# Gated attention's output projection and linear layer as three-pass products of split halves, the third norm on ScalarE, and two context buffers that swap homes

## The reference, cut to what matters

```python
# layer 2: gated linear attention
xb = silu(causal_conv(x)); q = xb @ Wq; k_gate = xb @ Wkg; v = xb @ Wv; g = xb @ Wg + bg
...
o = (o - mu) * lax.rsqrt(var + EPS)              # per head
out = jax.nn.silu(g) * o @ Wout                  # the output projection
# layer 3: linear layer with quantised operands, blocks of 32
xd = (xq * xs[..., None]).reshape(x2.shape)
wd = (wq * ws[..., None]).reshape(w2.shape)
out = xd @ wd.T + bias                           # the linear layer
# layer 4: cross attention, 16 heads
q = split(query @ Wq + bq); k = split(key @ Wk + bk); v = split(value @ Wv + bv)
...
x = x + layer(_layernorm(x, axis=-1))            # around each layer
```

## Time and profile before

| what | us |
|---|---|
| median of 3 runs (lowest, highest) | 1195.95 (1195.74, 1195.97) |
| the profiled execution's own time | 1191.81 |
| its span in the profile | 1190.5 |
| outside the span (1191.81 - 1190.5) | 1.3 |
| granted clock of PE over the span | 0.996 of full speed |
| PE, DVE, ACT, POOL busy | 1143.4, 744.6, 536.0, 236.7 |
| the loop: first scores to the end of the last linear product | 245.9 to 360.4 |

### The profile page before, as it was taken

One profiled execution on the slowest core, in us unless ns is written; L12 is line 12 of the kernel. 1 busy time (PEld: TensorE's weight loads), 2 busy tenths in 40 slices (PEclk: granted clock), 3 DMA queues, 4 the chain that ended last, 5 costly groups with the idle time before them and its releaser, 6 DMA issues.

```text
span 1190.5 us, 21697 instructions
## 1 busy us (share of the span) xinstructions
PE 1143.4 (96%) x8729; PEld 848.7 (71%) x8729; DVE 744.6 (63%) x1505; ACT 536.0 (45%) x1032; POOL 236.7 (20%) x292
## 2 busy tenths in 40 slices
PE   7999999989989999999999999999999999999997
PEld 5654477766547677777777777777787668887886
DVE  6457387678685665565566666665895767455632
ACT  3334346853212655555565656555553332223421
POOL 2300013066550061121212122211531100000000
PEclk9999999999999999999999999999999999999999
DMA  9759700110305155454444444454800402224211
GB/s 349 271 212 393 285 13 1 36 45 1 107 18 176 21 105 125 93 100 92 92 89 90 90 89 96 92 101 74 117 6 1 79 1 36 36 36 65 42 36 35
DMA packets 325671, 111.57 MB, mean 94 GB/s; under 512 B 301834, under 2 KB 302908, under 8 KB 321348
## 3 DMA queue, kind: packets, MB, share of 16 engines
q1 hardware_dynamic: 324224, 109.11, 36.5%
q10 hardware_dynamic: 1348, 1.09, 0.3%
HBM read 65.59 MB, written 20.97 MB: 73 GB/s over the span
## 4 chain that ended last, share of the span: by engine, by line
PE 84%; DVE 8%; ACT 4%; POOL 1%; issue 1%; DMA 1%; POOLq 0%; SPq 0%; DVEq 0%; ACTq 0%
PE bank L292 59%; PE bank L1845 3%; PE bank L1861 2%; PE bank L571 2%; PE bank L589 2%; PE bank L1152 2%; PE bank L1131 2%; PE bank L248 2%; DVE W L1394 1%; PE bank L507 1%; PE bank L238 1%; PE bank L1100 1%; PE bank L1084 1%; PE bank L1108 1%; PE bank L2268 1%
## 5 line engine op out<-in xcount | busy, mean ns | idle before, releaser
L1791 POOL COPY PT<-W 32x512 f32<-32x512 f32 x120 | 84.3, 703 | 311.3 <-DVE W L1984 246.3
L1973 DVE CUSTOM_DVE_ANT_0 W<-bank,W 128x512 f32<-128x512 f32 x128 | 80.8, 688 | 102.4 <-PE bank L1845 100.7
L2049 ACT ACTIVATE K<-bank,vecT 128x512 f32<-128x512 f32 x64 | 43.8, 690 | 166.9 <-PE bank L292 166.9
L2070 ACT ACTIVATE W<-W,low 128x512 f32<-128x512 f32 x128 | 90.7, 711 | 25.9 <-DVE low L1973 25.9
L292 PE MATMUL bank<-xT,wT 128*128 128x512 f32 x384 | 92.5, 390 | 0.8 <-ACT W L2933 0.5
L292 PE MATMUL bank<-Wkv,Wq 128*128 128x512 f32 x384 | 92.4, 395 | 0.0
L292 PE MATMUL bank<-Wkv,ctxT 128*128 128x512 f32 x384 | 91.8, 395 | 0.0
L292 PE MATMUL bank<-Wq,Wkv 128*128 128x512 f32 x384 | 89.9, 390 | 1.6 <-DVE Wq L309 1.6
L292 PE MATMUL bank<-ctxT,Wkv 128*128 128x512 f32 x384 | 89.8, 392 | 0.0
L292 PE MATMUL bank<-woT,hR 128*128 128x512 f32 x384 | 87.8, 390 | 0.7 <-DVE W_late L2854 0.5
L292 PEld LDWEIGHTS bank<-Wkv,ctxT 128*128 128x128 f32 x384 | 70.8, 188 | 22.2 <-ACT K L2049 5.7
(11 more groups left out here) (352 smaller groups left out, 2106.4 us busy)
## 6 DMA issues: line engine op xcount, KB each, us to landing
PT<-W SPq DMA_DIRECT2D x360, 64.0 KB, 2.1
W<-ctx_turned SPq DMA_DIRECT2D x16, 1024.0 KB, 5.7
W<-in_ctx_dram SPq DMA_DIRECT2D x8, 1024.0 KB, 10.1
ctx_turned<-ctxT SPq DMA_DIRECT2D x8, 1024.0 KB, 7.7
ctx_turned<-W SPq DMA_DIRECT2D x8, 1024.0 KB, 6.9
XT<-in_ctx_dram SPq DMA_DIRECT2D x4, 1024.0 KB, 12.0
XT<-in_L_ffn_wi_dram SPq DMA_DIRECT2D x64, 64.0 KB, 2.1
raw_own<-in_ctx_dram SPq DMA_DIRECT2D x3, 1024.0 KB, 11.2
```

What stands on the lines that cost most here:

```text
L1791: pool.tensor_copy(there, here).then_inc(kept_p.s, 1)
L1973: dve.tensor_tensor_reduce(out=PR[:, j, :], in0=bank[:, 4 + j % 4, :], in1=mask, scale=1.0, scalar=3.0e38, op0=ALU.add, op1=ALU.min, accum ...
L2049: act.activation(K[:, m, :], bank[:, n % 4, :], ACT.Identity, bias=pcol("L1_xattn_bk", m)).then_inc(ring_a.s, 1)
L2070: act.activation(PR[:, j, :], PR[:, j, :], ACT.Exp, bias=low[:, j:j + 1], scale=-1.0, accum_out=total[:, j:j + 1]).then_inc(expd.s, 1)
```

## The change

**Products.** The output projection and the linear layer become three-pass products of split halves. For y, ACT makes the high half (`y_high_a`, one buffer, so it waits for the projection before), POOL the low half in place of y (`y_low_pool`). For the turned blocks, ACT makes the high half straight from bank 6 and DVE the low half, also from bank 6 (`rows_low_v`, first in DVE's turn); the two halves fill the two places of xd. The waits on ACT's copy in widen, turn_blocks and linear become waits on DVE's low half. The weights' halves are made by ACT (4 copies before T1, 4 in T1), DVE (output projection, T1) and POOL (linear layer, T1 and T2).

**Order.** On PE the variance of a turn moves ahead of the projection. On POOL `y_low_pool(t-2)` stands ahead of bias and of the second norm's power. The key weights' halves move from T1 to T4 into T2 (two), T3 and T4. The query weights' low halves move from DVE to POOL, behind the loop.

**Third norm.** DVE no longer makes it; it only makes the negated mean, POOL multiplies that by the reciprocal deviation, and ACT applies both with one Identity activation per tile (`normalise_a`).

**Buffers.** Even contexts lie where `Wq` was, odd contexts and the query weights where `ctxT` was. A new buffer `WL` holds the low halves of the two weights.

```diff
@@ widen_pe, turn_blocks_pe, linear_pe
-                    pe.wait_ge(xt_a.s, xt_a(G + g - 3))
+                    pe.wait_ge(xt_v.s, xt_v(g - 3))
...
-                    pe.wait_ge(xt_a.s, xt_a(G + g - 1))
+                    pe.wait_ge(xt_v.s, xt_v(g - 1))
...
-                pe.wait_ge(xt_a.s, xt_a(G + g))
+                pe.wait_ge(xt_v.s, xt_v(g))
...
-                for c in range(C):
-                    ins = pe.matmul(bank[:, linear_at(g), :], xd[:, g % 2, c * P:(c + 1) * P], slot(8)[:, c, :], start=(c == 0), stop=(c == C - 1))
-                ins.then_inc(proj.s, 1)
+                product(bank[:, linear_at(g), :], lambda h, c: xd[:, h, c * P:(c + 1) * P], lambda h, c: Wlin[h][:, c, :],
+                        C).then_inc(proj.s, 1)
@@ project_pe
-                pe.wait_ge(ynm.s, ynm(g))
+                if g == 0:
+                    pe.wait_ge(wt_v.s, wt_v(15))
+                pe.wait_ge(low_w.s, low_w(C + g))
...
-                for c in range(C):
-                    ins = pe.matmul(bank[:, 7, :], y[:, g % 3, c * P:(c + 1) * P], slot(7)[:, c, :], start=(c == 0), stop=(c == C - 1))
-                ins.then_inc(proj.s, 1)
+                halves_of_y = (y_high, y_low[:, g % 3, :])
+                product(bank[:, 7, :], lambda h, c: halves_of_y[h][:, c * P:(c + 1) * P], lambda h, c: Wout[h][:, c, :],
+                        C).then_inc(proj.s, 1)
@@ gpsimd
                     if t <= G:
                         deviation_pool(t - 1)
+                    if t <= 2:
+                        for c in (2 * t - 2, 2 * t - 1):
+                            linear_weight_pool(c)
+                    if 2 <= t < G + 2:
+                        y_low_pool(t - 2)
                     if 4 <= t < G + 4:
                         bias_pool(t - 4)
                     if 3 <= t < G + 3:
                         row_stats_pool(2, t - 3)
+                for c in range(C):
+                    query_weight_pool(c)
...
+            def y_low_pool(g):
+                pool.wait_ge(high_w.s, high_w(g))
+                split_pool(y_low[:, g % 3, :], y[:, g % 3, :], y_high).then_inc(low_w.s, 1)
@@ tensor
+                    if 1 <= t <= G:
+                        variance_pe(t - 1)
                     if 3 <= t < G + 3:
                         project_pe(t - 3)
-                    if 1 <= t <= G:
-                        variance_pe(t - 1)
@@ vector
+            def rows_low_v(g):
+                dve.wait_ge(xt_a.s, xt_a(G + g))
+                split_v(xd[:, 1, :], bank[:, 6, :], xd[:, 0, :]).then_inc(xt_v.s, 1)
...
                 for t in range(G + 6):
+                    if 6 <= t:
+                        rows_low_v(t - 6)
                     if 3 <= t < G + 3:
                         normal_v(t - 3)
...
-                    if G + 4 <= t:
-                        for c in range(2):
-                            query_weights_v(2 * (t - G - 4) + c)
-                    if 7 <= t:
-                        normalise(xn4, 3, t - 7)
@@ scalar
+                for c in range(C):
+                    out_weights_a(c)
...
+                    if 3 <= t < G + 3:
+                        y_high_a(t - 3)
                     if 2 <= t < G + 2:
                         widen_a(t - 2)
...
+            def blocks_a(g):
+                if g:
+                    act.wait_ge(proj.s, proj(linear[g - 1]))
+                split_a(xd[:, 0, :], bank[:, 6, :]).then_inc(xt_a.s, 1)
...
+            def normalise_a(xn, g):
+                act.wait_ge(rstd_ok.s, rstd_ok(nth("rstd", 3, g)))
+                act.activation(xn[:, g, :], X[:, g, :], ACT.Identity, scale=rstd[:, g:g + 1],
+                           bias=shift[:, g:g + 1]).then_inc(kept["normed_a"].s, 1)
```

More of the change, by code:

```diff
@@ L114, in map_of_stages_4_and_5 @@
             first.close()
+            keep(first, "WL", "W_low", [P, 2, C, D], F32R)
+            first.close()
             keep(at, "bq", "bq5", [P, D])
@@ L123, in map_of_stages_4_and_5 @@
             keep(at, "Wo", "half_x", [P, 2, C, 512], F32R)
-            keep(second, "Wq", "Wq4", [P, 2, C, D], F32R)
+            keep(second, "ctxT_even", "ctxT_even", [P, 2, C, NK], F32R)
             keep(first, "half_x1", "half_x1", [P, 2, C, 512], F32R)
@@ L957, in l0_gated_attention @@
                         made[g] = G + 24 + len(out) + len(linear)
+            for l in (4, 5):
+                for g in range(G):
+                    side_by_side["normed", l, g] = (l - 1) * G + g
             summed = lambda l, g: xsum(nth("xsum", l, g))
@@ L1562, in blocks_a, with y_high_a, out_weights_a, linear_weights_a @@
                 act.wait_ge(turned.s, turned(2 * G + g))
-                if g >= 2:
-                    act.wait_ge(proj.s, proj(linear[g - 2]))
-                act.copy(xd[:, g % 2, :], bank[:, 6, :]).then_inc(xt_a.s, 1)
+                if g:
+                    act.wait_ge(proj.s, proj(linear[g - 1]))
+                split_a(xd[:, 0, :], bank[:, 6, :]).then_inc(xt_a.s, 1)
+            def y_high_a(g):
+                act.wait_ge(ynm.s, ynm(g))
+                if g:
+                    act.wait_ge(proj.s, proj(out[g - 1]))
+                split_a(y_high, y[:, g % 3, :]).then_inc(high_w.s, 1)
+            def out_weights_a(c):
+                act.wait_ge(slot_in[7].s, slot_in[7]())
+                split_a(Wout[0][:, c, :], slot(7)[:, c, :]).then_inc(wt_a.s, 1)
+            def linear_weights_a(c):
+                split_a(Wlin[0][:, c, :], slot(8)[:, c, :]).then_inc(wt_a.s, 1)
             def key_weights_a(c):
@@ L1663, in scalar @@
                             query_weights_a(c)
+                    if 7 <= t:
+                        normalise_a(xn4, t - 7)
             sync()
@@ L1886, in tensor @@
                         pe.wait_ge(xt_a.s, xt_a.base)
-                    transpose_rows(xn, 3, g, 4 + g % 3)
+                    pe.wait_ge(normed_a.s, normed_a(g))
+                    for c in range(C):
+                        ins = pe.transpose(bank[:, 4 + g % 3, c * P:(c + 1) * P], xn[:, g, c * P:(c + 1) * P], ident[:])
+                    ins.then_inc(turned.s, 1)
                     if g in (2, 5):
```

98 lines of the change are left out of this document (65 added, 33 removed).

## The result

The changed kernel takes 1225.98 us (median of 4 runs, 1223.09 to 1228.05) against 1195.85 (4 runs, 1189.42 to 1195.97): ratio 1.0275, 95% interval 1.0248 to 1.0303. The prediction said 1219.5, between 1204 and 1232, slower with a chance of 0.88. The profiled execution has a span of 1226.8 us, 36.3 more than before.

What follows compares the result with a forecast made beforehand. PE was taken to lead the loop, until new waits tie it and DVE into a ring. Ring 16.9, clock 4.9 and contention 2 sum to 23.8 us: 1215.6 for the profiled execution, 1219.5 at the median, range 1204 to 1232.

Steps and rivals of the forecast that it cites:

- The ring: Gated-attention and linear loop, where Tn is one pass: DVE and PE wait on each other, +16.9 us, bounds +13 to +21.
- the wait of the multiply for the widening transposes: DVE's multiply, every turn from T6: waits for PE's transposes right behind DVE's own low half, transposes about 0.5 us.
- the wait for the power: DVE's quantise norm, T8 to T10: waits for POOL's power behind y's low half, 2 to 4 us a turn.
- PE's gaps: Sign on PE in T9 to T12: idle gaps of 4 to 6 us with a granted clock below 1.00 behind them.
- The clock: PE's lowered clock after four gaps in T9 to T12: 4.9 us in sum, lower bound 0.
- the clock stays low: Rival for the loop: each step starts at the low clock and loses again; 1236 us, chance 0.06.
- The turns before T6: Loop's early turns: weight casts, variance order and POOL waits make DVE begin T6 at 296.0 us instead of 292.6.
- DVE against POOL: Contention slows DVE beside POOL: 0.5 us in each of T8 to T10, 0.8 in T5; 2 us, bounds 0 and 5.
- The splits of the output weights: DVE in T1 to T2: by the skill's rule each waits for a POOL split, some 3 us more, within slack.
- The query's low halves on POOL: nothing: Behind the loop: moving them from DVE to POOL costs nothing, covered before the query product; 5.1 us without that cover.
- After the loop: Later stages: every one as long as before; the prediction is wrong if that time changes by over 2 us.
- PE keeps the lead: Rival for the loop: DVE's low half is ready in time, 10.9 us saved less 3.7 lost; 1189 us, chance 0.08.

Runs made afterwards that it cites:

- experiment 4: Changed kernel plus 16 products that nobody reads at the head of each of PE's turns T9 to T13: 1217.36 us.
- Experiments 1: Changed kernel with DVE's low half of the turned rows made in the same turn, behind the variance, instead of first in the next: 1207.89 us.
- 2: Changed kernel with POOL's low half of y behind bias and the second norm's power instead of ahead of them: 1224.41 us.
- 6: Changed kernel with the projection back in float32, linear layer still three-pass, unneeded weight halves still made: 1224.33 us.
- Experiment 8: Changed kernel with early low half, y's low half behind bias and power, projection ahead of variance, ACT's carrier wait moved to its first exponential: 1204.25 us.
- experiment 10: Changed kernel with early low half, y's low half behind bias and power, carrier wait moved, unread products in PE's gaps: 1197.26 us.
- experiments 9: Changed kernel with linear layer in float32 without its splits, y's low half behind bias and power, projection before variance T3 to T5, carrier wait moved: 1196.07 us.
- 11: Changed kernel with float32 projection without its splits, early low half, projection before variance T3 to T5, key splits T1 to T3, carrier wait moved: 1196.15 us.
- twelfth experiment: Three-pass linear layer alone with mended orders, plus in T11 the low half ahead of the last quantise, context low halves a turn later: 1191.11 us.
- experiment 7: Changed kernel with both products back in float32, unneeded weight halves still made and not read: 1197.88 us.

## Why the prediction was right in sign and mechanism, and 6 us short

- **The size.** The medians are 6.5 us off. Execution against execution it is 12.4 (1228.05 against 1215.6): 3.0 ahead of the loop, 8.0 in the loop (31.8 against 23.8) and 1.5 behind it. The profiled execution of the kernel before was 4.0 us below its median and that of the changed one 2.1 above: that the medians hide half of the miss is luck. The sum has three slips that change nothing: T11 adds up to 8.7 and not 8.5, the contention to 2.3 and not 2, and 1215.6 with 4.1 is 1219.7.
- **The ring** was the likeliest case and it is what happened: the wait of the multiply for the widening transposes (1.27 us behind DVE's own low half), the wait for the power (3.78 us in T9), PE's gaps of 4.5 us. Its sizes hold where the clock is kept up (table under experiment 4). I gave its two waits equal weight, though. Experiments 1, 2 and 6 show that the first closes it, and that it holds the linear product as well as the projection; taking the second away by itself gave under 2 us.
- **The clock** is the term that was mis-sized. I took 4.9 us, in four gaps. T8 to T13 are 11.2 us longer than the predicted ring (66.3 against 55.1), of which contention was to be 1.5, and filling the gaps from T9 on gave back 8.6 us of median. Two steps of it failed. The clock also fell in T3, T8 and T13, behind waits of PE of 0.9 to 2.3 us, where I had counted nothing for it. And a product at the low clock takes 4.6 to 5.5 us, so 1.9 to 2.7 more than 2.76, not 1.4 to 1.9. The rival "the clock stays low" (1236) was wrong the other way: within each turn it came back, so the projection took 2.79 us behind a linear product of 5.03. The Trainium skill (TensorE: Matmul & The Clock Gate, HAM oscillation) describes a loop that waits in every step and starts each at the low clock, and the trace agrees in that. In its loop the work of a step is shorter than the wait; here PE works 9.3 us of a turn and waits 4.5.
- **The turns before T6.** I had DVE start T6 50.1 us after the first scores; it does so after 53.0. Of these 2.9 us the clock explains 1.7: the first projection took 4.5 us instead of 2.76, and DVE waited for it:

```profile
278.78 0.69 DVE L1389 TENSOR_TENSOR X<-X,bank 128x512 f32<-128x512 f32 x1 [5.33 <-PE bank L310]
```

  The other 1.2 us were not traced; the two long norms of T4 and T5, below, stand in this stretch, and POOL leads in it.
- **DVE against POOL** was foreseen in kind, and only in part in the right turns (T5 and T8 to T10). DVE's timeline of T4, T5 and T7 has the norm of 0.54 us at 1.49, 1.50 and 1.30, beside POOL's gating products at 284.88, 296.17 and 321.95:

```profile
284.95 1.49 DVE L250 TENSOR_SCALAR XT<-X,mv,rstd 128x512 f32<-128x512 f32 x1
...
296.24 1.50 DVE L250 TENSOR_SCALAR XT<-X,mv,rstd 128x512 f32<-128x512 f32 x1 [1.38 <-POOL rstd L236]
...
322.22 1.30 DVE L250 TENSOR_SCALAR XT<-X,mv,rstd 128x512 f32<-128x512 f32 x1
```

  In T8 to T10 it was 0.6 us once, and the quantising otherwise ran at its own speed. What it costs in all was not measured by itself. The splits of the output weights that the Trainium skill's rule (SBUF — State Buffer, Who interferes with whom) would have slowed ended at 262.3 us, before POOL's began at 263.3, so they show nothing of it. But the first of the four key-weight splits behind them, with both operands in SBUF, took 1.27 us instead of 0.68 beside POOL's gating product of 265.72 to 267.01, so there the trace agrees. The four together, against 2.51 us for those of the output weights:

```profile
266.29 3.10 DVE L327 TENSOR_TENSOR Wkv<-W,Wkv 128x512 fp32r<-128x512 f32 x4
```

- **"The query's low halves on POOL: nothing"** was wrong by 1.0 us. The cover I named was there; I had not asked who waits for the instruction queued behind them. Experiment 8 shows it.
- **After the loop** I allowed 2 us of change; it was 1.5, 1.0 of it the carrier.
- The 3.0 us ahead of the loop are no part of the change as far as these runs show: experiment 10 has its first scores at 245.91, with both clocks at 1.00. The kernel before has one profile only, so whether its executions start the loop earlier on average stays open. If they do, it would explain why experiments 9 and 11 are level in the stage and not in the median.
- "PE keeps the lead" (0.08, 1189) was not reached by any version with both products, the best of which took 1197.26 us. The mended kernel with the three-pass linear layer alone comes nearest: it is level with the kernel before.

## What to carry to other kernels

Count an operand's extra preparation by where it stands in the queue of the engine that makes it: 0.68 us of DVE at the head of its turn, with the waits and the low clock that it brought, took 18 us that went away when it stood in the turn of its own rows. When an engine is made to wait in every turn of a loop, price the clock of PE too, once for every gap: here filling them gave back 8.6 of the 30 us, and in one execution the clock fell after waits that the kernel before had as well. And for each instruction that is moved, ask who waits for what is queued behind it.

## What was not expected of the hardware

- The same code ran at different granted clocks from one execution to the next. In the stretch before the loop two windows of 40 us had 0.91 to 1.00, and the loop began up to 4.6 us apart. The runs of the kernel before alone spread over 9.9 us (1187.85 to 1197.74); of those beside the twelfth experiment the fastest, 1188.65 us, had a mean granted clock of 0.999, the slowest, 1197.74, one of 0.990.
- In experiment 7 and in the kernel before PE has the same waits of 1.18 us in T1 and T2. Before, the clock stayed at 1.00; in experiment 7 the second half of the attended values and the scores, in T2, took 2.08 and 1.76 us instead of 1.16 and 1.15 (PE's timeline of experiment 7):

```profile
260.51 2.08 PE L1145 MATMUL bank<-ident,XT 128*128 128x128 f32 x8
262.52 1.76 PE L1129 MATMUL bank<-W 32*128 32x256 f32 x16
```

- Sixteen products that nobody reads, at the head of each of PE's last five turns, made the kernel 8.6 us faster.
